# Attention denominators: sums on VectorE, one ones-product per chunk and head group, two context banks

## The chip, the cores and the metric

One core of one Trainium2 chip. The time is the device time of one execution in microseconds (us). Each of the eight sequences of the input ("batch" b below) runs through the whole layer; there is one launch.

## What is computed

For 8 sequences of 1,024 tokens and 256 features, in float32:

```
paths = sigmoid(x @ Wp + bp)                    # 8 heads x 5 values per token
agree = pq * pk + (1 - pq) * (1 - pk)           # per pair of tokens, head, depth
sim   = cumprod(agree, -1).sum(-1) / 5          # causal mask above the diagonal
attn  = softmax(sim, -1)
ctx   = attn @ V,  V = x @ Wv  (8 heads of 32)
x     = layernorm(x + ctx @ Wo)
h     = silu(x @ wg.T) * (x @ wu.T)             # hidden 768, integer weights / 127
x     = layernorm(x + h @ wd.T)
```

The similarity is a product of 32 features per token and head, so that the scores are a matmul. The softmax is written as exp without a maximum; its denominator is the sum of the probabilities over the keys.

## The kernel before

One list, `PLAN`, gives the order of all pieces of work. Each engine walks the same list and runs the pieces that are its own, in that order, and waits on semaphores. TensorE is PE, VectorE DVE, ScalarE ACT, GpSimd POOL.

Attention of a batch is 24 steps (`STEPS`). A step is one block of 128 keys (j) for one chunk of 512 queries (c) and one head group of 4 heads (g). The four pairs of chunk and group are q = 0 to 3: q 0 and q 1 (c = 0) have 4 steps each, i = 0 to 3 and 4 to 7; q 2 and q 3 (c = 1) have 8 each, i = 8 to 15 and 16 to 23. Only the queries from `off` on see a block: the four diagonal blocks of each chunk (`DIAG`) have 512, 384, 256 and 128 columns, the others 512.

Step s of the whole run (24 b + i) is planned as: `scores` (PE, L695) fills the two PSUM tiles `slot`; `exps` (ACT, L409) writes the probabilities of the 4 heads into one of three buffers `probs`; on the diagonal `mask` (POOL, L355) zeroes the 128 x 128 triangles; then come the pieces that `BETWEEN[i]` lists; then `weigh` for the step two before it (`LAG` = 2). `weigh` (PE, L717) has two groups of 4 matmuls, all over the same probabilities: the values `vz_sb` into `ctx_ps`, and a block of ones into `den_ps`, each head into its 32 partitions. After the last step of a q, `normalise` (DVE, L477 to L490) copies the context out of `ctx_ps`, transposes the denominators, takes the reciprocal, transposes back and multiplies into `ctxT`. So `normalise` stands in steps 5, 9, 17 and, for q 3, in step 1 of the next batch.

`BETWEEN` places the rest between the attention steps, one batch ahead (projections `vz`, `bias`, `squash`, `features`, `turn_f`, `phi` with `phi_low` on DVE) or one behind (`project` and `residual`, `stats` and `apply` of a layernorm with `rsqrt` on POOL, `turn_x1` with x1T_lo on DVE, the FFN's `gate`, `up`, `down`). A `gate_pair` is: gate (PE), tanh (ACT, L421), up (PE), and `hidden` on DVE, two instructions (L548, L556). `halves` is hid_hi (ACT, L427) and hidden_lo (POOL, L364), which `down` (PE, L762) waits for.

All PE pieces but scores and weighing write to two PSUM banks `misc` in turn. `MISC` numbers the uses in the order of `PLAN`, and a piece waits (`claim`) until its bank's last use is drained, mostly by a DVE instruction.

## Time and profile before

| | |
|---|---|
| median of 3 runs | 953.42 us (953.01 to 960.25) |
| the profiled execution, its own time | 955.83 us |
| its span, first to last instruction | 954.1 us |
| mean granted clock of TensorE | 0.969 |
| PE busy | 848.8 us, 89% |
| DVE busy | 478.6 us, 50% |
| ACT busy | 455.7 us, 48% |
| POOL busy | 227.4 us, 24% |

The busy times are of one profiled execution and are shares of its span. A busy PE is not PE at its peak: matmuls overlap, and their ends are modelled, so the cost of a group is read from its start to the start of what follows. PEclk is the granted clock as a share of 2.4 GHz; 0.5 is 1.2 GHz.

### The profile page before, as it was taken

What the parts mean: (1) busy time and instruction counts of PE and PEld (TensorE: products, weight loads), DVE (VectorE), ACT (ScalarE), POOL (GpSimd) and SP (SyncE); (2) the same over time, 40 slices, a digit from 0 to 9 for tenths busy, and PEclk for the clock granted to TensorE, in tenths of its full rate; (3) what the DMA queues carried; (4) which work ended last, traced back from release to release, by engine and by line L of the source; (5) the groups of instructions that cost most, each with busy time, mean ns of one, the idle gap of its engine ahead of it and who ended that gap; (6) DMA issues with size and microseconds to landing.
All of it is one profiled execution on the core that took longest, in us unless ns stands there. A gap on an engine that the chain in (4) does not pass through costs nothing.

```text
span 954.1 us, 15450 instructions
## 1 busy us (share of the span) xinstructions
PE 848.8 (89%) x6146; PEld 412.9 (43%) x6146; DVE 478.6 (50%) x1020; ACT 455.7 (48%) x721; POOL 227.4 (24%) x265
## 2 busy tenths in 40 slices
PE   4389998899989999899988999899988998999764
PEld 3144354443644446344544436344453434444332
DVE  2844346535455426645465355555275353545343
ACT  2255644555445554546445453555546453555211
POOL 0011131223212132122312232132321223231312
PEclk9599999999999999999999999999999999999968
DMA  6831443140511433113431406104321214100000
GB/s 211 213 97 45 89 89 111 45 90 23 141 59 45 111 66 107 72 43 70 89 111 45 89 23 152 70 23 111 82 74 45 64 48 109 47 1 23 1 22 24
DMA packets 44346, 71.09 MB, mean 75 GB/s; under 512 B 3568, under 2 KB 21232, under 8 KB 44272
## 3 DMA queue, kind: packets, MB, share of 16 engines
q1 hardware_dynamic: 44272, 70.07, 28.0%
q8 instruction: 51, 0.84, 0.4%
q14 instruction: 23, 0.19, 0.1%
HBM read 53.28 MB, written 16.78 MB: 73 GB/s over the span
## 4 chain that ended last, share of the span: by engine, by line
PE 73%; ACT 9%; DVE 9%; issue 4%; POOL 3%; DMA 2%; SPq 0%; POOLq 0%; ACTq 0%; DVEq 0%
PE ctx_ps L717 14%; PE misc L752 13%; PE den_ps L717 12%; PE slot L695 11%; PE misc L762 9%; PE misc L671 7%; PE misc L729 6%; ACT probs L409 6%; POOL work L364 2%; PE misc L680 2%; DVE work L548 2%; DVE x L531 1%; ACT work L421 1%; DVE ctx_raw L480 1%; DMA query_stack<-phi_dram 1%
## 5 line engine op out<-in xcount | busy, mean ns | idle before, releaser
L409 ACT ACTIVATE probs<-slot 128x1024 f32<-128x1024 f32 (+3 forms) x384 | 290.3, 808 | 376.4 <-PE slot L695 376.2
L695 PE MATMUL slot<-query_stack,key_stack 128*128 128x512 f16 (+3 forms) x768 | 161.7, 333 | 16.5 <-DMA query_stack<-phi_dram 15.1
L717 PE MATMUL ctx_ps<-probs,vz_sb 128*32 128x512 f32 (+3 forms) x1536 | 166.3, 505 | 10.3 <-DVE ctx_raw L480 8.3
L364 POOL TENSOR_TENSOR work<-work 128x512 f16<-128x512 f32 x96 | 112.7, 1174 | 216.0 <-ACT work L427 215.9
L717 PE MATMUL den_ps<-probs,ones 128*32 128x512 f32 (+3 forms) x1536 | 162.8, 495 | 0.0
L355 POOL TENSOR_SCALAR_AFFINE_SELECT probs<-probs 128x512 f32<-128x512 f32 x128 | 81.8, 641 | 303.9 <-ACT probs L409 302.9
L548 DVE SCALAR_TENSOR_TENSOR work<-work,misc 128x512 f32<-128x512 f32 x96 | 65.8, 686 | 172.7 <-ACT work L421 172.7
L752 PE MATMUL misc<-x1T_hi,w_parts 128*128 128x512 f16 x384 | 147.0, 383 | 5.2 <-DVE x1T_lo L538 2.4
L752 PE MATMUL misc<-x1T_lo,w_parts 128*128 128x512 f16 x384 | 146.5, 382 | 0.0
L695 PEld LDWEIGHTS slot<-query_stack,key_stack 128*128 128x128 f16 x768 | 56.8, 98 | 170.4 <-issue 120.9
L762 PE MATMUL misc<-w_parts,work 128*128 128x256 bf16 x768 | 89.1, 273 | 10.6 <-POOL work L364 10.6
L507 DVE SCALAR_TENSOR_TENSOR x<-misc,out_scale,x 128x512 f32<-128x512 f32 x32 | 24.0, 751 | 142.2 <-PE misc L762 142.2
L762 PEld LDWEIGHTS misc<-w_parts,work 128*128 128x128 f16 x768 | 73.7, 98 | 27.4 <-POOL work L364 16.4
L717 PEld LDWEIGHTS den_ps<-probs,ones 128*32 128x32 f32 x1536 | 50.2, 111 | 77.1 <-issue 68.1
L360 POOL TENSOR_TENSOR rstd<-var_eps,neg_half 128x4 f32<-128x4 f32 x32 | 32.4, 1013 | 193.7 <-DVE var_eps L525 193.7
L671 PE MATMUL misc<-wvp_sb,xT_sb 128*128 128x296 f32 x256 | 71.1, 425 | 7.3 <-DMA bp_sb<-in_bp_dram 7.3
L556 DVE SCALAR_TENSOR_TENSOR work<-work,hid_scale,misc 128x512 f32<-128x512 f32 x96 | 71.8, 748 | 3.8 <-PE misc L752 0.4
L729 PE MATMUL misc<-wo_sb,ctxT 128*128 128x256 f32 x256 | 60.9, 393 | 5.2 <-DVE ctxT L489 5.2
L421 ACT ACTIVATE work<-misc 128x512 f32<-128x512 f32 x96 | 57.8, 602 | 12.8 <-PE misc L752 12.8
L427 ACT ACTIVATE work<-work 128x512 f16<-128x512 f32 x96 | 61.3, 638 | 2.0 <-DVE work L556 2.0
L717 PEld LDWEIGHTS ctx_ps<-probs,vz_sb 128*32 128x32 f32 x1536 | 30.6, 108 | 72.5 <-issue 64.8
L752 PEld LDWEIGHTS misc<-x1T_hi,w_parts 128*128 128x128 bf16 x384 | 37.8, 98 | 55.7 <-DVE work L548 8.3
(52 smaller groups left out, 609.8 us busy)
## 6 DMA issues: line engine op xcount, KB each, us to landing
key_stack<-phi_dram SPq DMA_DIRECT2D x64, 256.0 KB, 5.8
query_stack<-phi_dram SPq DMA_DIRECT2D x64, 256.0 KB, 6.5
xT_sb<-in_xT_dram SPq DMA_DIRECT2D x8, 1024.0 KB, 5.1
x_sb<-in_x_dram SPq DMA_DIRECT2D x8, 1024.0 KB, 5.5
out_dram<-x SPq DMA_DIRECT2D x16, 512.0 KB, 2.9
phi_dram<-phi_hi SPq DMA_DIRECT2D x16, 256.0 KB, 2.0
phi_dram<-phi_lo SPq DMA_DIRECT2D x16, 256.0 KB, 2.3
work<-in_wgT_dram SPq DMA_DIRECT2D x1, 768.0 KB, 8.2
```

Of the source, the lines that this page charges most:

```text
L355: pool.affine_select(out=tile, in_=tile, compare_op=ALU.is_ge, fill=0.0, base=0, pattern=[[0, 4], [1, P]], channel_multiplier=-1).then_inc ...
L364: pool.tensor_tensor(hid_lo[:, n % M1, :], hid[:, n % HSLOTS, :], hid_hi[:, n % M1, :], ALU.subtract).then_inc(hid_lo_ready, 1)
L409: act.activation(probs[:, s % P_SLOTS, 2 * p:2 * p + 2, off:CH], slot[p][:, :, off:CH], ACT.Exp).then_inc(slot_drained[p], 1)
L421: act.activation(tanh_g[:, n % 2, :], misc[k][:, :], ACT.Tanh, scale=0.5 * QUANT).then_inc(tanh_ready, 1)
L548: dve.scalar_tensor_tensor(out=gated[:, n % 2, :], in0=tanh_g[:, n % 2, :], scalar=1.0, in1=misc[k][:, :], op0=ALU.add, op1=ALU.mult)\
L556: dve.scalar_tensor_tensor(out=hid[:, n % HSLOTS, :], in0=gated[:, n % 2, :], scalar=hid_scale[:, 0:1], in1=misc[k][:, :], op0=ALU.mult, o ...
L671: mm = pe.matmul(misc[k][:, 0:VZ], xT_sb[:, d, t * P:(t + 1) * P], wvp_sb[:, d, :], start=(d == 0), stop=(d == KD - 1))
L695: mm = pe.matmul(slot[p][:, k, off:CH], key_stack[:, h, P * j:P * (j + 1)], query_stack[:, h, CH * c + off:CH * (c + 1)], start=True, stop ...
L717: mm = pe.matmul(sums[32 * k:32 * k + 32, off:CH], w, probs[:, s % P_SLOTS, k, off:CH], start=first, stop=final)
L729: mm = pe.matmul(misc[k][:, (t % 2) * D:(t % 2 + 1) * D], ctxT[:, g, t * P:(t + 1) * P], wo_sb[:, g, :], start=(g == 0), stop=(g == NG - 1))
L752: mm = pe.matmul(misc[k][:, :], w_parts[:, w, e, d * F + m * P:d * F + (m + 1) * P], a[:, d, CH * c:CH * (c + 1)], start=(at == 0), stop=( ...
L762: mm = pe.matmul(misc[k][:, (t % 2) * D:(t % 2 + 1) * D], a[:, m, t * P:(t + 1) * P], w_parts[:, 2, e, m * D:(m + 1) * D], start=(at == 0) ...
```

## The change

- DVE gets a piece `sum` (`add_up`), planned in step s for the probabilities of step s - 1, ahead of the pieces of `BETWEEN`. The first sum of a q (j = 1) adds the probabilities of its first two steps into `acc` (on a diagonal step the columns below `off` are copied); each later one adds its step's to `acc`.
- PE's `weigh` loses the group over ones. A new piece `den`, behind the last weighing of a q, multiplies ones with `acc`, 4 matmuls into a `misc` bank; `normalise` transposes from there.
- `ctx_ps` becomes two banks, used in turn by q; the copy ctx_raw goes, and the last product of `normalise` reads `ctx_ps`.
- `exps` waits, beside `pv_done`, until the sum over the buffer that it overwrites is done.

```
@@ attention(s)
+        if 1 <= s <= B * NS:
+            plan += [("sum", *divmod(s - 1, NS))]
         plan += between(b, i)
         if LAG <= s < B * NS + LAG:
             b, i = divmod(s - LAG, NS)
-            plan += [("weigh", b, i)] + [("normalise", b, q) for q in range(NQ) if LAST[q] == i]
+            plan += [("weigh", b, i)]
+            for q in range(NQ):
+                if LAST[q] == i:
+                    plan += [("den", b, q), ("normalise", b, q)]
@@ the uses of misc
-        if what in ("scale", "vz", "turn_f", "project", "turn_x1", "gate", "up", "down"):
+        if what in ("scale", "vz", "turn_f", "project", "turn_x1", "gate", "up", "down", "den"):
@@ tiles
-        ctx_raw = sb("ctx_raw", [P, CH], F32)
+        acc = sb("acc", [P, 4, CH], F32)
-        ctx_ps = ctx.enter_context(nc.psum_tensor("ctx_ps", [P, CH], F32))
-        den_ps = ctx.enter_context(nc.psum_tensor("den_ps", [P, CH], F32))
+        ctx_ps = [ctx.enter_context(nc.psum_tensor(f"ctx_ps{n}", [P, CH], F32)) for n in range(2)]
@@ exps (ACT)
                     act.wait_ge(pv_done, s - P_SLOTS + 1)
+                    b2, i2 = divmod(s - P_SLOTS, NS)
+                    act.wait_ge(summed, SUMMED[b2, i2 + (STEPS[i2][3] == 0)])
@@ DVE
+            def add_up(b, i):
+                q, c, g, j = STEPS[i]
+                if j == 0:
+                    return
+                off = max(P * j - CH * c, 0)
+                s = NS * b + i
+                own = probs[:, s % P_SLOTS, :, off:CH]
+                if i in DIAG:
+                    dve.wait_ge(masked, len(DIAG) * b + DIAG.index(i) + 1)
+                else:
+                    for p in range(2):
+                        dve.wait_ge(slot_drained[p], s + 1)
+                if j == 1:
+                    if NQ * b + q >= 1:
+                        k, n = MISC[("den", *divmod(NQ * b + q - 1, NQ))]
+                        dve.wait_ge(misc_filled[k], n + 1)
+                    first = probs[:, (s - 1) % P_SLOTS, :, :]
+                    if off:
+                        dve.tensor_copy(acc[:, :, 0:off], first[:, :, 0:off]).then_inc(summed, 1)
+                    dve.tensor_tensor(acc[:, :, off:CH], first[:, :, off:CH], own, ALU.add).then_inc(summed, 1)
+                else:
+                    dve.wait_ge(summed, SUMMED[b, i] - 1)
+                    dve.tensor_tensor(acc[:, :, off:CH], acc[:, :, off:CH], own, ALU.add).then_inc(summed, 1)
@@ normalise (DVE)
-                dve.wait_ge(pv_done, NS * b + LAST[q] + 1)
-                if Q >= 1:
-                    dve.wait_ge(ctxT_ready, Q)
-                dve.tensor_copy(ctx_raw[:, :], ctx_ps[:, :]).then_inc(ctx_out, 1)
-                dve.transpose(den_turned[:, :, :].rearrange("p a n -> p (a n)"), den_ps[:, :]).then_inc(den_out, 1)
-                dve.wait_ge(den_out, Q + 1)
+                k, n = MISC["den", b, q]
+                dve.wait_ge(misc_filled[k], n + 1)
+                dve.transpose(den_turned[:, :, :].rearrange("p a n -> p (a n)"), misc[k][:, :])\
+                    .then_inc(misc_drained[k], 1)
+                dve.wait_ge(misc_drained[k], n + 1)
...
-                dve.wait_ge(ctx_out, Q + 1)
-                dve.tensor_tensor(ctxT[:, g, :], ctx_raw[:, :], den_inv[:, :], ALU.mult)\
+                dve.wait_ge(pv_done, NS * b + LAST[q] + 1)
+                dve.tensor_tensor(ctxT[:, g, :], ctx_ps[q % 2][:, :], den_inv[:, :], ALU.mult)\
@@ weigh and denominator (PE)
-                for sums, taken in ((ctx_ps, ctx_out), (den_ps, den_out)):
-                    if first and NQ * b + q >= 1:
-                        pe.wait_ge(taken, NQ * b + q)
-                    for k in range(4):
-                        h = 4 * g + k
-                        w = vz_sb[:, b % 2, j, 32 * h:32 * h + 32] if taken is ctx_out else ones[:, :]
-                        mm = pe.matmul(sums[32 * k:32 * k + 32, off:CH], w,
-                                       probs[:, s % P_SLOTS, k, off:CH], start=first, stop=final)
+                if first and NQ * b + q >= 2:
+                    pe.wait_ge(ctxT_ready, NQ * b + q - 1)
+                for k in range(4):
+                    h = 4 * g + k
+                    mm = pe.matmul(ctx_ps[q % 2][32 * k:32 * k + 32, off:CH],
+                                   vz_sb[:, b % 2, j, 32 * h:32 * h + 32],
+                                   probs[:, s % P_SLOTS, k, off:CH], start=first, stop=final)
                 mm.then_inc(pv_done, 1)
+
+            def denominator(b, q):
+                pe.wait_ge(summed, SUMMED[b, LAST[q]])
+                n = claim("den", b, q)
+                for k in range(4):
+                    mm = pe.matmul(misc[n][32 * k:32 * k + 32, :], ones[:, :], acc[:, k, :], start=True, stop=True)
+                mm.then_inc(misc_filled[n], 1)
```

`SUMMED` counts the increments of `summed` up to each step.

## Rows read from the trace of the kernel before

**Rows 1.** The page, part 1: busy us (share of the span) xinstructions.
```profile
PE 848.8 (89%) x6146; PEld 412.9 (43%) x6146; DVE 478.6 (50%) x1020; ACT 455.7 (48%) x721; POOL 227.4 (24%) x265
```
**Rows 2.** The page, part 4: the chain that ended last, by engine.
```profile
PE 73%; ACT 9%; DVE 9%; issue 4%; POOL 3%; DMA 2%; SPq 0%; POOLq 0%; ACTq 0%; DVEq 0%
```
**Rows 3.** Windows: batch 4 (steps 0-5, 6, 7-10, 11-14, 15-23), then batch 5.
```profile
core 0: us, PE busy (x) PEld busy (x) DVE busy (x) ACT busy (x) POOL busy (x), PEclk, DMA share, GB/s
461.34:489.43 28.09, 27.89 (x220) 17.61 (x216) 14.64 (x41) 12.00 (x21) 6.99 (x10) 1.00 0.52 131
489.43:497.70 8.27, 5.80 (x40) 2.61 (x37) 6.91 (x15) 3.56 (x7) 0.64 (x1) 0.84 0.38 127
497.70:516.76 19.06, 16.59 (x124) 6.89 (x120) 9.91 (x15) 11.46 (x17) 3.79 (x4) 0.98 0.15 56
516.76:535.20 18.44, 18.44 (x125) 8.42 (x121) 9.37 (x23) 9.98 (x15) 5.82 (x8) 1.00 0.00 1
535.20:573.05 37.85, 36.52 (x281) 15.59 (x277) 16.17 (x33) 19.69 (x30) 11.01 (x12) 1.00 0.31 73
573.05:683.11 110.06, 103.60 (x772) 50.78 (x769) 57.28 (x124) 56.68 (x90) 28.21 (x33) 1.00 0.30 77
```
**Rows 4.** Timeline of PE, batch 4: ahead of turn_features (step 6) and down (15).
```profile
493.39 1.22 PE L680 MATMUL misc<-ident,feat 128*128 128x128 f32 x8 [2.47 <-DVE x1T_lo L538]
...
536.29 2.79 PE L762 MATMUL misc<-w_parts,work 128*128 128x256 bf16 x24 [0.69 <-POOL work L364]
```
**Rows 5.** Timeline of PE: weighing of 128 and of 512 columns.
```profile
511.64 0.43 PE L717 MATMUL ctx_ps<-probs,vz_sb 128*32 128x128 f32 x8
511.88 0.40 PE L717 MATMUL den_ps<-probs,ones 128*32 128x128 f32 x8
...
514.91 1.06 PE L717 MATMUL ctx_ps<-probs,vz_sb 128*32 128x512 f32 x8
515.79 1.04 PE L717 MATMUL den_ps<-probs,ones 128*32 128x512 f32 x8
```
**Rows 6.** Groups by form, VectorE's longest tensor_tensor: busy us, mean ns | idle before.
```profile
L583 DVE TENSOR_TENSOR work<-work,w_parts 128x1536 f32<-128x1536 int32 x3 | 5.2, 1748 | 0.0
```
**Rows 7.** Timeline of VectorE in batch 4: statistics, normalise, apply, phi_low, hidden.
```profile
470.45 1.40 DVE L520 BATCH_NORM_STATS2 bn<-x 128x6 f32<-128x256 f32 x4
...
472.37 0.69 DVE L480 COPY ctx_raw<-ctx_ps 128x512 f32<-128x512 f32 x1
...
475.36 1.38 DVE L531 TENSOR_SCALAR x<-x,mv,rstd 128x256 f32<-128x256 f32 x4
...
512.47 0.75 DVE L470 SCALAR_TENSOR_TENSOR phi_lo<-misc,feat_scale,phi_hi 128x512 f16<-128x512 f32 x1 [0.75 <-ACT phi_hi L398]
...
530.94 0.75 DVE L556 SCALAR_TENSOR_TENSOR work<-work,hid_scale,misc 128x512 f32<-128x512 f32 x1
...
548.20 0.69 DVE L548 SCALAR_TENSOR_TENSOR work<-work,misc 128x512 f32<-128x512 f32 x1 [1.38 <-ACT work L421]
548.92 0.75 DVE L556 SCALAR_TENSOR_TENSOR work<-work,hid_scale,misc 128x512 f32<-128x512 f32 x1
...
570.03 0.75 DVE L556 SCALAR_TENSOR_TENSOR work<-work,hid_scale,misc 128x512 f32<-128x512 f32 x1
```
**Rows 8.** Mask and hidden_lo on GpSimd; hidden_lo beside a product of VectorE (timeline).
```profile
L355 POOL TENSOR_SCALAR_AFFINE_SELECT probs<-probs 128x512 f32<-128x512 f32 x128 | 81.8, 641 | 303.9 <-ACT probs L409 302.9
...
L364 POOL TENSOR_TENSOR work<-work x96: 1152/1162/1643, 107.7 to 938.9; 128x512 f16<-128x512 f32 x96
...
836.15 0.69 DVE L489 TENSOR_TENSOR ctxT<-ctx_raw,den_inv 128x512 f32<-128x512 f32 x1
836.22 1.64 POOL L364 TENSOR_TENSOR work<-work 128x512 f16<-128x512 f32 x1 [2.11 <-ACT work L427]
```
**Rows 9.** Timeline of batch 0: scores of step 4, end of the weights' split.
```profile
54.71 1.04 PE L695 MATMUL slot<-query_stack,key_stack 128*128 128x512 f16 x4
...
56.12 0.17 DVE L621 COPY w_one<-w_gmax 128x2 f32<-128x2 f32 x1 [1.54 <-issue]
```

More of the change, by code:

```diff
@@ L153, in seq_postln_kernel @@
             misc_uses[k] += 1
+    SUMMED, pieces = {}, 0
+    for b in range(B):
+        for i in range(NS):
+            q, c, g, j = STEPS[i]
+            pieces += (0, 2 if c == 0 else 1)[j >= 1] if j <= 1 else 1
+            SUMMED[b, i] = pieces
     NORM = {tuple(n): at for at, n in enumerate([n for what, *n in PLAN if what == "stats"])}
@@ L245, in seq_postln_kernel @@
         pv_done = sem("pv_done")
-        ctx_out = sem("ctx_out")
-        den_out = sem("den_out")
+        summed = sem("summed")
         den_recip_ready = sem("den_recip_ready")
@@ L472, in phi_low @@
                                          op0=ALU.mult, op1=ALU.subtract).then_inc(misc_drained[k], 1)
+            def add_up(b, i):
+                q, c, g, j = STEPS[i]
+                if j == 0:
[19 more added lines that the diff above has]
+                    dve.tensor_tensor(acc[:, :, off:CH], acc[:, :, off:CH], own, ALU.add).then_inc(summed, 1)
             def normalise(b, q):
@@ L633, in _ @@
                     split_weights()
+                elif what == "sum":
+                    add_up(*n)
                 elif what == "normalise":
@@ L779, in walk @@
                         weigh(*n)
+                    elif what == "den":
+                        denominator(*n)
                     elif what == "project":
```

## The prediction

> **What bounds the kernel now.** The page's busy times come first: TensorE is busy 849 of 954 us, VectorE half as long [rows 1], and the chain that ended last is 73% TensorE [rows 2]. That says where a removed instruction may pay, not how much. So I cut one batch in the middle of the run at the starts of score groups and read PE and DVE side by side [rows 3]. In steps 0 to 5 PE stops for 0.2 us, in steps 6 to 10 it stands still for 4.9 us, then it is nearly full again. The batch takes 111.7 us, the next one 110.1 us. The 1.6 us between them is low clock: steps 6 to 10 show a granted clock of 0.84 and 0.98 (of 2.4 GHz; a mix of 2.4 and 1.2), right behind PE's stop of 2.47 us, and the next batch shows 1.00 throughout. PE's stops name their releasers [rows 4]: the long one VectorE's x1T_lo, the one ahead of down GpSimd's hidden_lo. So PE sets the pace, but it runs through a ring of two `misc` banks, and VectorE, in program order, frees most of them. The change moves work from the first engine to the second.
>
> **What is removed on PE.** A full denominator group (4 heads of 512 columns) delays what follows as the context group ahead of it does, 515.79 - 514.91 = 0.88 us; one of 128 columns 0.24 us [rows 5]. On the line between them 384 columns cost 0.67 and 256 cost 0.45 us. A batch has 12 groups of 512 and 4 of each other size: 10.6 + 2.7 + 1.8 + 1.0 = 16.0 us. Added are four groups over `acc`, 4 x 0.88 = 3.5 us. Net 12.5 us a batch, 100 us in all, if nothing else came late.
>
> **What is added on DVE.** No row shows a tensor_tensor of 4 x 512. Two inputs in SBUF take 1,748 ns for 1,536 elements (L583) and 0.69 us for 512 (L489) [rows 6, 8]: 1.03 ns per element, so 2.28 us for 2,048, and 1.75, 1.22 and 0.69 us in the diagonal steps. A successor starts 0.03 to 0.09 us before the listed end [rows 7], so I use 2.25, 1.67, 1.15 and 0.62. Bounds of a full sum: 2.11 us at 1.03 ns without any start-up, 2.76 us at four times the 512-element row. I take the line, since the 1,536 row is nearest. The short head copy (512 elements) lies between half the 512 row, 0.35, and 0.69 us; I take 0.35, it is small either way. A batch has eight full sums, four of each shorter size and two copies: 18.0 + 6.7 + 4.6 + 2.5 + 0.7 = 32.5 us. Removed are four copies of ctx_raw at 0.6, 2.4 us. The final product now reads PSUM; the copy L480, as long, out of PSUM takes the same 0.69 us as L489 out of SBUF [rows 7, 8], so nothing. DVE goes from 57.3 us a batch [rows 3] to 87.4 us, PE from 103.6 to 91.1 us. The two become nearly equal, and where DVE's part of a step is longer than PE's, DVE sets the pace.
>
> **Where this lands in a batch.** I walked the batch in program order on both engines, always taking the later of "engine free" and "bank or data there" (0.1 us for a hand-over and 0.9 us where a tanh lies between are estimates). Start of a score group in us from the batch's own start, before [rows 3] and after:
> - Step 6: 28.1, after 28.0. Weighing loses 0.45, 0.24, 0.88, 0.67, 0.45, 0.24, and two denominators add 1.76: -1.2. Down of step 0 comes earlier on PE than hidden_lo on its chain of ACT and GpSimd: 1 us more of waiting. In step 2 the second `vz` wants the denominator's bank, which DVE's transpose frees only behind the layernorm statistics: a new stop of 0.85. Smaller hand-overs differ by -0.7.
> - Step 7: 36.4, after 35.3. PE waits for x1T_lo. DVE comes to it behind the normalise and, newly, behind the sum of step 5 (0.35 + 1.67): the stop grows from 2.5 to 3.7. Weighing loses 0.88, and the low clock no longer costs, as DVE is 2 us behind PE there.
> - Step 11: 55.4, after 52.9. Weighing loses 0.67, 0.45, 0.24 and 0.88, the second denominator adds 0.88; the rest is what the shorter `normalise` gives back.
> - Step 15: 73.9, after 71.5. This stretch becomes DVE's. From the end of phi_low (512.47 + 0.75) to the end of `hidden` of step 13 (530.94 + 0.75) it took 18.5 us with gaps [rows 7]. After: normalise 3.0 - 0.6 = 2.4, four full sums 9.0, three pairs of `hidden` at 0.72 + 0.66 = 4.1, residuals 1.2, statistics 1.9, apply 1.3 and 0.4 of hand-overs: 20.3 us without a gap. PE saves 3.5 us of weighing from step 11 to 15 and waits it all again, 1.4 us at step 11, 0.7 and 1.8 at steps 13 and 14.
> - End: 111.7, after 106.7. Steps 15 to 17 save 2.2 on weighing against 0.88 for the denominator and 0.9 more of waiting for hidden_lo. Then DVE again: from hidden(0) (548.92 + 0.75) to hidden(5) (570.03 + 0.75) it took 21.1 us [rows 7]; after it is apply 1.3, normalise 2.4, sums 9.0 + 1.67, five pairs 6.9 = 21.3 us. PE's saving there only brings the batch's end closer behind DVE's.
> So of 12.5 us removed, 3.4 us (110.1 to 106.7) remain against a batch without low clock, 4.2 against the mean of both.
>
> **The port.** GpSimd's hidden_lo, 1.16 us as a rule, took 1.64 us when it began 0.07 us behind L489, a VectorE product of two SBUF tensors, and L489 kept its 0.69 us [rows 8]. The second to come waited. Every sum is such an instruction. Mostly hidden_lo and mask will wait for the sum and then run beside `hidden`, which reads PSUM, at no cost. In the diagonal steps 20 to 22 and in 14 mask and hidden_lo are both queued behind the sum, 0.64 + 1.16 = 1.8 us against the pair's 1.4: the next sum waits 0.3 us, four times, and the last hidden_lo reaches down by so much later: 1.5 us a batch with its own waiting. The batch becomes 108.2 us.
> The Trainium skill says this outright ("SBUF — State Buffer", section "Who interferes with whom"): a VectorE instruction with two SBUF inputs and a GpSimd instruction that reads SBUF share an interface, and the later one blocks fully. By that rule, the trace agrees; were there no such lock, the batch would be 106.7 and the forecast 10 us lower.
>
> **The other edits.** Two context banks: the waits for ctx_raw at a new chunk go, but DVE sets the pace around them, so I take nothing for it; were they all on the path, it would be 1 us a batch. `exps` also waits for the sum of three steps back, and with it the next scores: late by 1.2 us at step 19, still ahead of PE's need. In batch 0 it costs: DVE splits weights until 56.3 us [rows 9]; the sum of step 1 ends at 58.3, exps(3) at 59.0, scores(4) starts at 59.1 instead of 54.7. The weighing saved in that batch outweighs these 4.4 us; I take -3 us for batch 0, between 0 and -8. Behind the last batch only a copy falls away, -0.6 us. More stops mean more low clock: at 1.6 us a period, mostly under DVE's work, I add 0.5 us a batch.
>
> **Sum.** Seven batches x (108.2 - 110.9) = -19, batch 0 -3, tail -0.6, clock +3.5: -19 us. The profiled execution took 955.8 us (span 954.1 and 1.7 around it), which gives 936.7. It lies 2.4 us above the median of the runs shown, so 953.4 - 19 = 934 us.
>
> **Rivals.**
> - *PE stays the bound* and DVE keeps up everywhere: 953 - 100 = 853 us. For it: a DVE that is half idle today. Against: the two stretches of 41.6 us have no room on DVE by rows. Chance 0.03. In part (sums at 2.11 us, no port waits) it gives 905 to 920: chance 0.05.
> - *The clock takes it back.* Stops of 1.4 to 1.9 us appear at steps 11, 14, 15 and 18 beside the 3.7. The stop of 2.47 us was followed by low clock in this batch and not in the next. If two such periods a batch are not covered, that is +3.2 us x 7, less the 3.5 counted: 953 us, no change. Chance 0.23.
> - *The port makes it slower.* One mechanism: in the eight steps that DVE bounds the sum finds hidden_lo (1.16 us) at the port, because hid_hi leaves ACT just ahead of the sum and not during it. Then GpSimd's time joins DVE's own chain: 8 x 1.0 us a batch, 934 + 7 x 8 = 990 us. It decides for slower from 4 us of such waits a batch. Against: ACT does exp and tanh first, so hid_hi ends some 0.5 us before the sum does. Chance 0.14.
> - That a denominator group stays in `weigh` is excluded by the diff, so the change does what it says.
>
> **Chances and range.** Forecast (920 to 944) 0.55, more gain 0.08, clock 0.23, port 0.14. A measurement of this kernel tells 1% (9.5 us) from no change. Faster by over 1%, below 943.9: 0.63; within 1%: 0.23; slower: 0.14. The range 914 to 963 leaves out the slower case and the free PE.
>
> **What would show it.** In the changed profile: PE busy down by some 100 us, DVE up by 230 to 240 us to about 715; a full sum at 2.28 us; steps 10 to 13 and 18 to 22 with DVE over 95% busy and PE waiting at `misc` for L548's product; the stop ahead of turn_features in step 6 at 3.7 us behind x1T_lo; batches of 107 to 110 us; hidden_lo often at 1.5 us and more; scores(4) of batch 0 near 59 us. Wrong it would be by sums much over 2.3 us, by DVE idle in those steps (then the ring binds, not the load), or by sums that start long after both inputs while GpSimd is busy.

## The result and the profile after

The changed kernel takes 978.18 us (median of 4 runs, 974.59 to 981.85) against 954.24 us for the kernel before beside it (953.01 to 960.25): 1.0238 times as long, 95% interval 1.018 to 1.0296. The forecast was 934 us in a range of 914 to 963; the change makes the kernel slower by 2.4%, 24 us, where 19 us of gain were forecast.

The page of the changed kernel, busy times and the chain that ended last by engine, which answer to [rows 1] and [rows 2]:
```profile
PE 793.5 (81%) x4866; PEld 379.8 (39%) x4866; DVE 737.0 (75%) x1164; ACT 459.7 (47%) x721; POOL 327.3 (34%) x265
...
PE 46%; DVE 21%; issue 11%; ACT 10%; POOL 9%; DMA 2%; SPq 0%; DVEq 0%; ACTq 0%; POOLq 0%
```
PE gave up 55 us and DVE took 258 us. What was not expected stands at the end of the first line: GpSimd runs the same 265 instructions and is busy 100 us longer. In the chain PE lost 27 points of share; DVE has 12 more, POOL 6 and "issue" 7.

The groups of GpSimd in the changed kernel show where the 100 us are:
```profile
L374 POOL TENSOR_TENSOR work<-work 128x512 f16<-128x512 f32 x96 | 145.3, 1514 | 208.8 <-ACT work L440 208.5
L365 POOL TENSOR_SCALAR_AFFINE_SELECT probs<-probs 128x512 f32<-128x512 f32 x128 | 132.5, 1037 | 244.2 <-ACT probs L422 244.2
L370 POOL TENSOR_TENSOR rstd<-var_eps,neg_half 128x4 f32<-128x4 f32 x32 | 51.1, 1597 | 182.7 <-DVE var_eps L563 159.2
```
hidden_lo took 1,162 ns in the median and mask 641 in the mean [rows 8]; now their means are 1,514 and 1,037. The reciprocal root of a layernorm works on 4 elements per partition; its mean was 1,013 ns and is 1,597 ns.

Windows over the changed kernel, in the same steps of batch 4 as [rows 3] (columns as there):
```profile
471.20:502.60 31.40, 28.77 (x189) 17.36 (x185) 20.94 (x47) 12.64 (x22) 9.88 (x11) 0.95 0.48 119
502.60:511.40 8.80, 5.07 (x32) 2.52 (x28) 7.53 (x13) 3.67 (x7) 0.64 (x1) 0.83 0.31 116
511.40:529.10 17.70, 15.19 (x101) 5.99 (x98) 12.69 (x19) 11.47 (x17) 3.14 (x3) 0.99 0.16 59
529.10:549.30 20.20, 17.27 (x93) 7.50 (x90) 19.74 (x29) 10.21 (x15) 13.11 (x8) 0.92 0.00 1
549.30:583.65 34.35, 31.46 (x216) 13.27 (x213) 28.16 (x39) 19.25 (x29) 15.39 (x11) 1.00 0.34 78
```
Against [rows 3], steps 0 to 5 take 3.3 us more, steps 11 to 14 1.8 us more with DVE busy 98% of them, and only steps 7 to 10 and 15 to 23 are shorter (by 1.4 and 3.5 us). Cut at the starts of score groups, batch 0 is 7.0 us longer than before (93.8 for 86.8), batches 1 to 6 together 9.3 us (674.6 for 665.3, so 112.4 each for 110.9), batch 7 up to its last scores 1.4 us, and what follows them, the tail, 5.2 us (67.7 for 62.5): 22.9 us, with the first scores 0.1 us earlier. The two spans differ by 22.8 us.

PE's longest waits in the changed kernel (us in total, times, longest):
```profile
PE misc L720 <- DVE x1T_lo L576: 22.4, 6, 3.7
PE misc L808 <- POOL work L374: 22.2, 14, 3.2
PE misc L784 <- DVE work L586: 17.1, 7, 2.9
PE misc L798 <- DVE work L586: 15.8, 20, 1.4
```

### The profile page after: what moved, and what is told of

It reads as the page before. It is cut to its first block, busy times and chain, and to the rows that moved or that the text cites. A ratio compares the mean times of both kernels' runs of the same rounds, so it can differ in the third digit from the quotient of the medians.

```text
span 976.9 us, 13193 instructions
## 1 busy us (share of the span) xinstructions
PE 793.5 (81%) x4866; PEld 379.8 (39%) x4866; DVE 737.0 (75%) x1164; ACT 459.7 (47%) x721; POOL 327.3 (34%) x265
## 4 chain that ended last, share of the span: by engine, by line
PE 46%; DVE 21%; issue 11%; ACT 10%; POOL 9%; DMA 2%; SPq 0%; DVEq 0%; ACTq 0%; POOLq 0%
PE misc L808 9%; PE ctx_ps L755 8%; ACT probs L422 7%; PE slot L735 7%; PE misc L711 6%; PE misc L798 6%; PE misc L775 5%; POOL probs L365 5%; DVE acc L508 4%; DVE work L586 4%; POOL work L374 3%; DVE x L569 2%; DVE acc L511 2%; DVE bn L558 2%; PE misc L720 2%
## 5 line engine op out<-in xcount | busy, mean ns | idle before, releaser
L511 DVE TENSOR_TENSOR acc<-acc,probs 128x2048 f32<-128x2048 f32 (+3 forms) x128 | 221.4, 1730 | 5.3 <-POOL probs L365 4.8
L374 POOL TENSOR_TENSOR work<-work 128x512 f16<-128x512 f32 x96 | 145.3, 1514 | 208.8 <-ACT work L440 208.5
L365 POOL TENSOR_SCALAR_AFFINE_SELECT probs<-probs 128x512 f32<-128x512 f32 x128 | 132.5, 1037 | 244.2 <-ACT probs L422 244.2
L755 PE MATMUL ctx_ps<-probs,vz_sb 128*32 128x512 f32 (+3 forms) x1536 | 175.4, 531 | 2.6 <-POOL probs L365 2.6
L808 PE MATMUL misc<-w_parts,work 128*128 128x256 bf16 x768 | 98.6, 290 | 22.4 <-POOL work L374 22.2
L370 POOL TENSOR_TENSOR rstd<-var_eps,neg_half 128x4 f32<-128x4 f32 x32 | 51.1, 1597 | 182.7 <-DVE var_eps L563 159.2
L586 DVE SCALAR_TENSOR_TENSOR work<-work,misc 128x512 f32<-128x512 f32 x96 | 65.4, 681 | 42.0 <-ACT work L434 42.0
L808 PEld LDWEIGHTS misc<-w_parts,work 128*128 128x128 f16 x768 | 78.5, 104 | 44.1 <-POOL work L374 28.3
L711 PE MATMUL misc<-wvp_sb,xT_sb 128*128 128x296 f32 x256 | 75.1, 438 | 10.8 <-DMA bp_sb<-in_bp_dram 7.0
L798 PEld LDWEIGHTS misc<-x1T_hi,w_parts 128*128 128x128 bf16 x384 | 38.1, 99 | 83.1 <-DVE work L586 31.9
L508 DVE TENSOR_TENSOR acc<-probs 128x1536 f32<-128x1536 f32 (+1 forms) x32 | 64.5, 2017 | 0.0
L711 PEld LDWEIGHTS misc<-wvp_sb,xT_sb 128*128 128x128 f32 x256 | 49.8, 202 | 31.1 <-DMA bp_sb<-in_bp_dram 7.1
```

The lines of the kernel that those rows point to most:

```text
L365: pool.affine_select(out=tile, in_=tile, compare_op=ALU.is_ge, fill=0.0, base=0, pattern=[[0, 4], [1, P]], channel_multiplier=-1).then_inc ...
L374: pool.tensor_tensor(hid_lo[:, n % M1, :], hid[:, n % HSLOTS, :], hid_hi[:, n % M1, :], ALU.subtract).then_inc(hid_lo_ready, 1)
L508: dve.tensor_tensor(acc[:, :, off:CH], first[:, :, off:CH], own, ALU.add).then_inc(summed, 1)
L511: dve.tensor_tensor(acc[:, :, off:CH], acc[:, :, off:CH], own, ALU.add).then_inc(summed, 1)
L586: dve.scalar_tensor_tensor(out=gated[:, n % 2, :], in0=tanh_g[:, n % 2, :], scalar=1.0, in1=misc[k][:, :], op0=ALU.add, op1=ALU.mult)\
L711: mm = pe.matmul(misc[k][:, 0:VZ], xT_sb[:, d, t * P:(t + 1) * P], wvp_sb[:, d, :], start=(d == 0), stop=(d == KD - 1))
```

## The experiments

All ratios are to the kernel before, run beside each. Its medians there were 954.3 to 955.8 us.

**What DVE's time costs, and what the port costs.** *One input.* The sums become reductions over the same number of elements, which read one SBUF tensor; the denominators are left out of the result (the matmul over ones reads a constant `acc`). The main line of the edit:
```
-dve.tensor_tensor(acc[:, :, off:CH], acc[:, :, off:CH], own, ALU.add).then_inc(summed, 1)
+dve.tensor_reduce(junk[:, 0:4], own, AX.X, ALU.max).then_inc(summed, 1)
```


> Each sum becomes a tensor_reduce over as many elements of the same buffer, with one input and a tiny output, so the denominators are left out (ones times a constant). VectorE's time and order stay (1,753 ns against 1,748 ns for 1,536 elements in the kernel before); the second SBUF input goes. Theory port (the sums keep GpSimd from the SBUF, and what GpSimd is late with stops down, apply and the next sum): mask, rsqrt and hidden_lo go back to 0.64, 1.01 and 1.16 us, the stop ahead of down in step 0 falls from 2 us to about 1, 925 to 950 us. Theory load (VectorE's 32 us more a batch, in program order, is enough): 970 to 985 us, as the changed kernel.

Measured: 953.59 us, ratio 0.9981 (0.9965 to 0.9997), 4 us above the range of theory port and 16 us below that of theory load. A reduction takes as long as a sum: its timeline row for 2,048 elements beside the one of the changed kernel, each with the reciprocal root that comes right behind it. The changed kernel (VectorE, then GpSimd, step 12 of batch 4):
```profile
537.37 2.29 DVE L511 TENSOR_TENSOR acc<-acc,probs 128x2048 f32<-128x2048 f32 x1
...
537.51 3.02 POOL L370 TENSOR_TENSOR rstd<-var_eps,neg_half 128x4 f32<-128x4 f32 x1 [2.57 <-DVE var_eps L563]
```
With one input (the same two, same step):
```profile
524.41 2.29 DVE L514 TENSOR_REDUCE junk<-probs 128x4 f32<-128x2048 f32 x1
...
524.55 1.01 POOL L372 TENSOR_TENSOR rstd<-var_eps,neg_half 128x4 f32<-128x4 f32 x1 [3.40 <-DVE var_eps L566]
```
GpSimd's groups of that kernel:
```profile
L376 POOL TENSOR_TENSOR work<-work 128x512 f16<-128x512 f32 x96 | 111.2, 1158 | 238.6 <-ACT work L442 237.8
L367 POOL TENSOR_SCALAR_AFFINE_SELECT probs<-probs 128x512 f32<-128x512 f32 x128 | 85.8, 671 | 279.7 <-ACT probs L424 279.7
L372 POOL TENSOR_TENSOR rstd<-var_eps,neg_half 128x4 f32<-128x4 f32 x32 | 32.4, 1012 | 190.9 <-DVE var_eps L566 167.4
```
Started 0.14 us behind a sum, the root stood until about the sum's end and then took its own time; behind a reduction it ran beside it. GpSimd is back near its old times, and 25 us are gone (978.2 to 953.6; by the two intervals 17 to 32). The reduction differs from the sum in its output too, 4 elements per partition for up to 2,048. That the second SBUF input is what counts shows in the changed kernel itself: 14 masks that began during the transpose den_inv (L523, one SBUF input, 512 columns written to SBUF) took 0.64 us, and the 7 hidden_lo that began during x1T_lo (L576, one input in SBUF and one in PSUM) took their 1.16 us. Masks that began during a `tensor_scalar` over SBUF (L569) took up to 0.85 us; that is open.

VectorE is held in its turn. DVE is busy 737.0 us in the change and 712.4 us here: some sums began while GpSimd was at work and took longer. In step 14 of batch 5 of the changed kernel (GpSimd, VectorE, PE):
```profile
655.12 1.16 POOL L374 TENSOR_TENSOR work<-work 128x512 f16<-128x512 f32 x1 [0.32 <-ACT work L440]
...
655.18 3.24 DVE L511 TENSOR_TENSOR acc<-acc,probs 128x2048 f32<-128x2048 f32 x1
...
659.17 1.08 PE L784 MATMUL misc<-ident,x 128*128 128x128 f32 x4 [2.90 <-DVE work L586]
```
The product of L586 stands behind that sum, and PE waits 2.90 us for it. Batches 2, 3, 5 and 6 are like this; in batches 1, 4 and 7 hidden_lo comes behind the sum, and PE's stop is 1.84 us, as with one input.

*No sums.* Each becomes a `memset` of one column; denominators left out.
```
+dve.memset(junk[:, 0:1], 0.0).then_inc(summed, 1)
```


> The changed kernel with each sum replaced by a memset of one column: the denominators are left out, TensorE's saving stays, VectorE's cost goes. If TensorE's 12.5 us a batch were simply on the path: 853 to 865 us. If GpSimd's and ACT's chains come next (hidden_lo ahead of down, x1T_lo): 870 to 895 us.

Measured: 885.96 us, 0.928 (0.9242 to 0.9319). So what PE gives up, with the second bank, is worth 69 us, and DVE's time takes 68 of them back, before the port (885.96 against 953.59).

*Sums that nobody reads*, added to the kernel before, with the wait of `exps`; its ones-groups and its one context bank stay. The line of the plan (the piece itself is that of the change):
```
+if 1 <= s <= B * NS:
+    plan += [("sum", *divmod(s - 1, NS))]
```


> The kernel before, with the sums beside it that nobody reads (and the wait of exps for them); the result is the reference's. Theory load: the same stretches become VectorE's with no saving on TensorE, 985 to 1000 us, far less than adding the two effects, since TensorE is hidden where VectorE bounds. If VectorE's cost and TensorE's saving add up (both all on the path): 978 + (954 - the time without sums), some 1050 to 1070 us.

Measured: 1042.97 us, 1.0907 (1.0879 to 1.0935), 87 us over the kernel before beside it, 7 us short of the range expected for adding up (1050 to 1070) and far from the other (985 to 1000). Had the two engines shared the load as a maximum, PE's untouched work would have covered a good part of that. It covered some 5 us at most: 978 us and the 69 us of PE's and the bank's saving make 1047. Costs on DVE and savings on PE add up almost as on one serial chain.

**Where the port hurts.** *Mask last*: the mask goes behind the pieces of `BETWEEN`, and so behind GpSimd's `hidden_lo` and root of its step. In the change it stands ahead of them, and in step 0 ahead of the split of the weights.
```
-if i in DIAG:
-    plan += [("mask", b, i)]
...
 plan += between(b, i)
+if b < B and i in DIAG:
+    plan += [("mask", b, i)]
```


> The changed kernel with GpSimd's mask planned behind the pieces of BETWEEN, so that hidden_lo and rsqrt of a step run ahead of it; nothing is left out. Theory port with the queue on GpSimd: hidden_lo of the last gate no longer stands behind a mask that a sum holds up, the stop ahead of down in step 0 falls from 2.0 to about 1.0 us, 966 to 973 us. Theory load: 975 to 982 us, or slower where the next sum waits for the later mask.

Measured: 968.18 us, 1.0133 (1.0101 to 1.0164). The 10 us come from batch 0 (93.8 to 89.2 us) and the tail (67.7 to 62.5, its length before the change); batches 1 to 6 keep their mean of 112.4.

The gain in batch 0 is not the port's. GpSimd also takes a maximum that DVE's split of the weights waits for (`w_gmax`), from values that DVE finishes at 45.6 us in both kernels. Planned behind mask(0) (44.04 to 44.68 us), it starts 8.2 us after that mask; planned ahead of it, as soon as DVE's values are there. First the changed kernel, then this one:
```profile
52.89 0.39 POOL L386 PARTITION_ALL_REDUCE w_gmax<-w_max  x1 [8.21 <-issue]
...
45.79 0.39 POOL L386 PARTITION_ALL_REDUCE w_gmax<-w_max  x1 [44.01 <-DVE w_max L627]
```
What GpSimd does in those 8.2 us the profile does not name ("issue"); the kernel before has such a gap too (7.4 us). So DVE is done with the weights 7 us earlier, the sums of q 0 end at 54.4 us and not at 61.5, and scores(4) starts at 54.69 us, as before the change.

In the changed kernel the tail begins so (GpSimd, then PE, timeline):
```profile
910.50 1.62 POOL L365 TENSOR_SCALAR_AFFINE_SELECT probs<-probs 128x512 f32<-128x512 f32 x1
912.09 1.15 POOL L374 TENSOR_TENSOR work<-work 128x512 f16<-128x512 f32 x1
...
913.29 0.94 PE L808 MATMUL misc<-w_parts,work 128*128 128x256 bf16 x7 [2.95 <-POOL work L374]
```
The sum of step 22 (910.21, 1.41 us) holds the mask of 0.64 us, `hidden_lo` stands behind it, and `down` behind that. The same order of events stands at every batch's start: in batch 5 GpSimd's rows and then PE's are
```profile
583.87 1.62 POOL L365 TENSOR_SCALAR_AFFINE_SELECT probs<-probs 128x512 f32<-128x512 f32 x1
585.47 1.15 POOL L374 TENSOR_TENSOR work<-work 128x512 f16<-128x512 f32 x1
...
586.67 4.46 PE L808 MATMUL misc<-w_parts,work 128*128 128x256 bf16 x24 [1.98 <-POOL work L374]
```
and `down` then runs at the low clock, 4.46 us for the 2.79 of [rows 4]. PE's stop there is 1.98 us in each of batches 1 to 7, 0.86 us with one input and 1.70 us with the mask last: with the mask out of the way the sum of step 22 holds `hidden_lo` itself (1.75 us in batch 5). So of the 1.1 us that the port adds to this stop, the queue behind the mask is 0.3. The low clock follows the stop in batches 2, 4 and 5 alone, where step 0 takes 8.0 us and not 6.3.

Means over batches 1 to 6 of the time from score group to score group, in us, put the places side by side:

| | before | change | one input | mask last | filled stops |
|---|---|---|---|---|---|
| step 0 | 4.96 | 7.15 | 5.19 | 6.03 | 6.32 |
| steps 1 to 5 | 23.13 | 23.39 | 23.40 | 24.16 | 23.40 |
| step 6 | 7.69 | 8.58 | 8.92 | 8.97 | 9.09 |
| steps 7 to 10 | 18.82 | 17.99 | 17.90 | 18.50 | 18.59 |
| steps 11 to 13 | 15.16 | 14.06 | 14.04 | 14.05 | 14.05 |
| step 14 | 3.27 | 6.71 | 5.78 | 5.15 | 5.85 |
| steps 15 to 23 | 37.85 | 34.53 | 34.39 | 35.52 | 35.24 |
| batch | 110.9 | 112.4 | 109.6 | 112.4 | 112.6 |

The port's 2.8 us a batch are 2.0 in step 0 and 0.9 in step 14. Mask last shortens the same two steps by 2.7 us together and loses as much in steps 5, 6, 7 and 15 to 23.

*Both last*: mask and sum behind the pieces, three buffers.
```
 plan += between(b, i)
+if b < B and i in DIAG:
+    plan += [("mask", b, i)]
+if 1 <= s <= B * NS:
+    plan += [("sum", *divmod(s - 1, NS))]
```


> Both changes of order together, mask and then sum behind the pieces of BETWEEN; nothing is left out. Theory place and port: the gains add, 930 to 948 us, which would beat the kernel before (954). Theory amount: 972 to 985 us.

Measured: 979.25 us, 1.0252 (1.0221 to 1.0282), no better than the change. With three buffers `exps` waits for the later sums (143 us in the run for 77), as in "sum last" below.

**The clock.** PE's time at the low clock (1.2 GHz) rose from 62 to 133 us; the mean granted clock fell from 0.969 to 0.933. *Filled stops*: 8 matmuls into the idle context bank ahead of `down` in step 0 and of `turn_x1` in step 14.
```
+def keep_busy(bank, done, times=8):
+    pe.wait_ge(ctxT_ready, done)
+    for n in range(times):
+        pe.matmul(ctx_ps[bank][:, :], w_parts[:, 0, 0, 0:P], w_parts[:, 1, 0, 0:CH], start=True, stop=True)
```


> The changed kernel with eight matmuls of 128x512 bf16 into the idle context bank ahead of the waits of down (step 0) and turn_x1 (step 14), 1.7 us in stops of about 2 us. Theory clock (the stops cost twice, because low clock follows them: the down group behind the stop took 4.46 instead of 2.79 us): low clock falls from 133 us to about 90 us in the run, 958 to 966 us. Port and load alone: 975 to 985 us.

Measured: 973.46 us, 1.0161 (1.0105 to 1.0218). The low clock is gone at both places. In step 14 of batch 4 `turn_x1` now runs at the full clock, and then PE waits anyway (PE's timeline):
```profile
541.83 1.89 PE L783 MATMUL ctx_ps<-w_parts 128*128 128x512 bf16 x8
544.90 0.63 PE L791 MATMUL misc<-ident,x 128*128 128x128 f32 x4 [1.18 <-DVE work L586]
...
548.75 2.79 PE L817 MATMUL misc<-w_parts,work 128*128 128x256 bf16 x24 [1.12 <-POOL work L374]
```
Batches 1 to 6 are not shorter (112.6 us for 112.4): steps 0 and 14 are 1.7 us shorter together, and steps 6 to 10 and 15 to 23 longer by 1.8. The 5 us in the median are within the two intervals. But the run did not take the low clock away. It came back behind step 6: the granted clock of that step of batch 4 is 0.76 for 0.83, and of the first 4 us of step 7 0.70. In all 119 of the 133 us at the low clock are left, where about 90 were expected. So this run does not show what the low clock costs.

**The wait of `exps`.** *Four buffers* of `probs` instead of three; `den_inv` shares `den_turned`'s memory to make room.
```
-P_SLOTS = 3
+P_SLOTS = 4
```


> The changed kernel with four buffers of probabilities instead of three, so that exps waits for the sum of four steps back; two denominator tiles share memory to make room. In the changed kernel ACT stands 77 us behind sums. Theory exps (these waits hold up the scores and so TensorE): 945 to 962 us. Port and load: no change beyond 5 us but for batch 0, whose 5 us of waiting behind the split weights shrinks: 970 to 978 us.

Measured: 978.88 us, 1.0241 (1.021 to 1.0272). Batch 0 becomes 90.0 us for 93.8, so the wait costs 3.9 us once; batches 1 to 6 and the tail stay. Batch 7 is 4.5 us longer up to its last scores (104.3 for 99.8), in steps 0, 3, 7 and 14; why is open.

*Sum last*: the sum goes behind the pieces, the mask stays.
```
-if 1 <= s <= B * NS:
-    plan += [("sum", *divmod(s - 1, NS))]
 plan += between(b, i)
+if 1 <= s <= B * NS:
+    plan += [("sum", *divmod(s - 1, NS))]
```


> The changed kernel with each step's sum planned behind the pieces of BETWEEN instead of ahead of them; nothing is left out. Theory place (the sum costs where it stands ahead of a piece that frees misc: x1T_lo in step 6, the gate products in steps 11 to 14 and 19): the stop ahead of turn_features falls from 3.7 to about 1.7 us and the one of step 14 by as much, 940 to 955 us. Theory amount (VectorE is full, it matters not which piece waits): 972 to 985 us.

Measured: 1010.66 us, 1.0579 (1.0544 to 1.0615). The waits of `exps` for sums, first in the changed kernel, then in this one:
```profile
ACT probs L422 <- DVE acc L508: 48.4, 25, 8.6
ACT probs L422 <- DVE acc L511: 28.9, 8, 4.2
```
```profile
ACT probs L422 <- DVE acc L508: 113.1, 31, 6.2
ACT probs L422 <- DVE acc L511: 58.4, 25, 7.4
```
The stretch of step 6, which had lost time to a sum ahead of x1T_lo, did shrink (5.5 us for 8.8), but `exps` waits 172 us for 77, and batches 1 to 6 take 115.9 us for 112.4. Most of that is step 0, 10.7 us for 7.2.

**The second context bank.** *One bank* and the copy ctx_raw again, all else changed.
```
+dve.tensor_copy(ctx_raw[:, :], ctx_ps[:, :]).then_inc(ctx_out, 1)
```


> The changed kernel with one context bank and the copy ctx_raw back in normalise; nothing is left out. It measures the part of the change that the forecast took for nothing: 976 to 984 us. Rival (the second bank and the missing copy are worth 1 us a batch and more, since VectorE is full): 986 to 995 us.

Measured: 1005.0 us, 1.0523 (1.0506 to 1.0541): 27 us slower than the change and above both expected ranges. Against the sums that nobody reads (1042.97 us, one bank as well) it is 38 us faster: that is what the removed denominator groups alone are worth beside the sums.

Batches 1 to 6 take 116.2 us for 112.4, and 2.7 of the 3.8 us are in step 19 (580.43 to 588.45 in batch 4, 8.0 us for 5.3). VectorE, then GpSimd, then PE in it:
```profile
577.10 0.68 DVE L522 COPY ctx_raw<-ctx_ps 128x512 f32<-128x512 f32 x1
...
580.09 3.25 DVE L510 TENSOR_TENSOR acc<-probs 128x2048 f32<-128x2048 f32 x1
583.26 0.67 DVE L592 SCALAR_TENSOR_TENSOR work<-work,misc 128x512 f32<-128x512 f32 x1
...
580.00 1.18 POOL L376 TENSOR_TENSOR work<-work 128x512 f16<-128x512 f32 x1 [5.44 <-ACT work L442]
...
583.99 0.39 PE L804 MATMUL misc<-x1T_hi,w_parts 128*128 128x512 f16 x1 [2.52 <-DVE work L592]
```
The copy puts 0.6 us into DVE's queue, the sum behind it begins 0.09 us behind a `hidden_lo` and takes 1.0 us longer than its 2.28, and PE's gate, which needs the product of L592 behind it, waits 2.5 us for 1.4. What follows is at the low clock; the window of step 19 here and then in the change:
```profile
580.43:588.45 8.02, 5.50 (x25) 1.38 (x21) 7.95 (x7) 3.06 (x4) 2.13 (x2) 0.79 0.01 2
...
566.29:571.60 5.31, 3.87 (x24) 1.17 (x21) 5.27 (x4) 2.95 (x4) 3.16 (x2) 1.00 0.01 3
```
From the gate's start to the next scores it is 4.5 us for 2.8: of the 2.7 us, 1.1 are the wait and 1.6 the rows at the low clock behind it. In the changed kernel the same first sum of a pair took 2,283 ns in the mean of 16, here 2,705.

**A better order.** *Four buffers, both last*: the two edits of "both last" and "four buffers" together.
```
-P_SLOTS = 3
+P_SLOTS = 4
...
 plan += between(b, i)
+if b < B and i in DIAG:
+    plan += [("mask", b, i)]
+if 1 <= s <= B * NS:
+    plan += [("sum", *divmod(s - 1, NS))]
```


> Mask and sum behind the pieces of BETWEEN, and four buffers of probabilities, so that the late sum no longer stops exps (172 us of waiting with three); nothing is left out. Theory place: with exps free the order helps, 940 to 958 us. Theory amount (VectorE's 32 us cost two thirds of what TensorE saves wherever they stand): 970 to 985 us.

Measured: **943.06 us**, 0.9865 (0.9847 to 0.9882), faster than both kernels. Windows over the same steps of batch 4:
```profile
450.85:483.48 32.63, 28.98 (x189) 17.27 (x185) 22.59 (x48) 12.52 (x22) 12.15 (x12) 0.95 0.48 116
483.48:488.98 5.50, 3.77 (x33) 2.19 (x29) 4.29 (x8) 3.51 (x7) 0.64 (x1) 1.00 0.43 170
488.98:508.13 19.15, 15.29 (x100) 5.75 (x97) 15.26 (x24) 11.51 (x18) 2.96 (x3) 1.00 0.15 56
508.13:525.48 17.35, 15.57 (x93) 7.24 (x89) 16.61 (x25) 9.98 (x15) 9.47 (x6) 1.00 0.00 0
525.48:559.43 33.95, 31.27 (x216) 13.44 (x212) 30.02 (x42) 19.46 (x30) 16.18 (x11) 1.00 0.36 80
```
Steps 6 and 11 to 14 are 3.3 and 2.9 us shorter than in the change and stay at the full clock; steps 0 to 5 are still the long ones (32.6 us for 28.1 before).

Four more tell what carries it. *Four buffers, sum last* (the mask in its old place):


> The changed kernel with four buffers and the sum last, the mask in its old place; nothing is left out. Theory place with exps as what stopped the late sum: four buffers are enough, 943 to 952 us. Theory port (the mask ahead of hidden_lo is held up by the sum and holds up down): 955 to 970 us.

Measured: 972.9 us, 1.0197 (1.0143 to 1.025), above both expected ranges. So the mask's place is worth 30 us here: 3.2 us in each of batches 1 to 6, above all in steps 0 and 14, and 5.3 us in the tail. *The kernel before with four buffers*, and *with four buffers and the mask last*:


> The kernel before with four buffers of probabilities and nothing else. Control for the version with both orders and four buffers (943 us): if that gain is the change's, given the right place, 950 to 958 us here; if the fourth buffer itself brings it, 938 to 948 us.

> The kernel before with four buffers and GpSimd's mask behind the pieces of BETWEEN; nothing is left out. Second control: 948 to 958 us if neither buffer nor order of GpSimd helps a kernel without sums; 938 to 946 us if hidden_lo ahead of mask brings down (0.2 to 0.7 us of waiting per batch) and more forward.

Measured: 955.37 us, 1.0007 (0.9991 to 1.0022), and 953.01 us, 0.9991 (0.9968 to 1.0013). Neither the buffer nor both together are worth anything without the sums, so the 1.35% are the change's own. *The better order with one-input sums* (denominators left out, as above):


> The version with both orders and four buffers, its sums replaced by tensor_reduce with one SBUF input (the denominators are left out). What is left of the port in it: theory port, 12 to 25 us, 918 to 931 us, with the stop ahead of down in step 0 back under 1.5 us; rival (the new order already keeps sums and GpSimd apart): 937 to 944 us.

Measured: 909.02 us, 0.953 (0.95 to 0.9559): the port still costs 34 us in the better order, more than the 12 to 25 expected.

**Fewer sums.** From the kernel before (one context bank, `den_ps` kept): sums for part of the steps, the others keep their ones-group. *q 0 and the first five steps of q 3*, then *the first five of q 3 alone*. The steps of each q that are summed:
```
+M = {0: 4, 1: 0, 2: 0, 3: 5}
...
+M = {0: 0, 1: 0, 2: 0, 3: 5}
```


> From the kernel before: VectorE sums only the four steps of q 0 and the first five of q 3, and one product over the sum takes the place of their ones groups; q 1, q 2 and the last three steps of q 3 keep theirs; one context bank and the copy stay. TensorE loses 4.9 us a batch, VectorE gains 13. Theory map (a sum costs only where it stands ahead of x1T_lo or a gate product that TensorE waits for: steps 6, 11, 14 and, for 1.6 us, 19): 936 to 946 us, faster than before. Theory amount (every us on VectorE costs 0.33 us, every us off TensorE gives 0.7): 960 us.

> As the one with q 0 and q 3, but only the first five steps of q 3: TensorE loses 3.5 us a batch, VectorE gains 9. Theory map: 2.6 us saved less 1.6 at step 19, 944 to 950 us. Theory amount: 957 to 961 us.

Measured: 972.18 us, 1.016 (1.0131 to 1.0188), and 963.7 us, 1.0085 (1.0057 to 1.0113). Both were placed where the one-input and the no-sums kernel, compared step by step, had shown little cost of DVE's time, and both lose, each by more than either theory had expected. In the second, step 19 of batch 4 takes 9.5 us for the 4.7 before, with PE in front of a gate:
```profile
559.33 0.61 PE L811 MATMUL misc<-x1T_hi,w_parts 128*128 128x512 f16 x1 [3.06 <-DVE work L593]
```
DVE there does `normalise`, a sum and only then the product that frees the bank, and the gate runs at the low clock. With this fell the idea that a half-idle DVE makes a sum free, even in chosen steps. Whether another choice of steps would gain was not tried.

## Why the prediction was wrong

The forecast lay 44 us below the result, 42 if the spans are compared. By the score groups, 26 of these are in batches 1 to 7 (112.4 us each where 108.7 were forecast, the 0.5 for the clock included), 10 in batch 0 and 6 in the tail. The steps that failed are the port, batch 0, the tail, and the low clock behind step 6; the bank was mis-sized in the good direction. By its own steps:

**The second bank, "I take nothing for it", "1 us a batch" at most.** Bank and copy together are worth 27 us beside the sums. The copy's own time, 2.4 us of DVE a batch, was in the walk; for the rest I took nothing, since I bounded it by the waits for ctx_raw in the trace of before, where no sum stood beside the copy on DVE. This error hides a part of the others: without bank and copy the change would have been at 1005 us. How the 27 us divide into the copy's time, PE's wait, the collision and the low clock was seen in step 19 and not measured apart.

**The port, 1.5 us a batch.** The mechanism was right, its size was not, and its place only in part. It cost 25 us between the medians and 23 us between the spans (976.9 against 953.7) where the sum had 10: 3.9 in batch 0 and 3.0 in the tail, for both of which I had nothing, and 16.9 in batches 1 to 6, 2.8 each. I looked for it in steps 14 and 20 to 22, where DVE sets the pace. Step 14 has 0.9 us of it, steps 20 to 22 0.2. The larger part, 2.0 us, is at the seam of two batches, where DVE is not the bound at all: the sum of step 22 holds mask(23) and hidden_lo, PE has nothing else in its order and waits for the last hidden_lo at `down` in step 0 (1.98 us for 0.86), and in batches 2, 4 and 5 it then runs `down` at the low clock. I had written the sentence ("the last hidden_lo reaches down by so much later") and given it a share of 1.5 us. And I had left GpSimd's root out: I thought of it as 4 elements, but at a locked port what counts is what is left of the other's instruction, here up to 2.3 us. Every GpSimd instruction of the profile before was a candidate; I priced hidden_lo and mask, in five steps.

The Trainium skill ("SBUF — State Buffer", section "Who interferes with whom") calls the shared ports an exclusive lock. By that rule, the trace agrees: 3.02 us for the root, 3.25 us for the sum in the one-bank kernel, each its own time (1.01 and 2.28) and about what was left of the other's (2.15 and 1.09).

**DVE sets the pace from step 11 on.** Right. DVE's chain from phi_low's end to `hidden` of step 13 was 20.3 us in the sum and is 20.46 in the one-input kernel (from 512.80 to 533.26), from hidden(0) to hidden(5) it was 21.3 and is 21.4 in the change (562.24 to 583.67); full sums are 2.28 us where nothing holds them, DVE is busy 98% in steps 11 to 14 (97% in steps 10 to 13, 99% in 18 to 22), and PE waits at `misc` for the product of L586. DVE's busy time without the port is 712.4 us (forecast 715).

**"The low clock no longer costs" behind step 6.** Wrong, and it is the largest part of what is left. Without the port the walk had 106.7 us a batch and the one-input kernel takes 109.6. Its windows over the same steps of batch 4:
```profile
460.93:489.53 28.60, 27.10 (x189) 16.50 (x185) 19.59 (x46) 12.62 (x22) 7.69 (x10) 1.00 0.53 131
489.53:498.48 8.95, 5.11 (x32) 2.54 (x29) 7.63 (x13) 3.67 (x7) 0.64 (x1) 0.83 0.35 114
498.48:516.14 17.66, 15.14 (x100) 6.03 (x97) 12.18 (x19) 11.47 (x17) 3.13 (x3) 0.99 0.16 59
516.14:536.29 20.15, 17.23 (x93) 7.49 (x89) 19.68 (x29) 10.21 (x15) 7.14 (x8) 0.92 0.00 1
536.29:570.45 34.16, 31.51 (x216) 13.34 (x213) 27.25 (x39) 19.30 (x30) 9.94 (x11) 1.00 0.34 78
```
The walk had 28.0, 7.3, 17.6, 18.6 and 35.2. Two stretches are longer, step 6 by 1.65 and steps 11 to 14 by 1.55 us, and both hold the low clock (0.83 and 0.92). In step 6 PE stops for 3.73 us in the changed kernel, as forecast (3.7), and then:
```profile
507.95 1.68 PE L720 MATMUL misc<-ident,feat 128*128 128x128 f32 x8 [3.73 <-DVE x1T_lo L576]
509.56 1.94 PE L755 MATMUL ctx_ps<-probs,vz_sb 128*32 128x512 f32 x8
```
The weighing had 1.06 us in [rows 5]. ScalarE and DVE turn to phi only when turn_features ends, so its slowness is on DVE's path as well. I had argued that DVE was 2 us behind PE there; at that point DVE waits for PE. In steps 11 to 14 the rows at the low clock stand behind PE's last stop; DVE does not wait there, and the next stretch is 1.0 us shorter than the walk had it, so little of those 1.55 us reaches the batch. That the low clock costs some 1.3 us in step 6 is read from these rows (1.68 us for 1.22, 1.94 for 1.06), not from a run that removed it alone; no filler was tried in step 6.

**Batch 0, -3.** It was +7.0. Scores(4) starts at 59.55 us (forecast 59.1, before 54.71), so the wait of `exps` was sized well; a fourth buffer gives back 3.9 us and one-input sums 3.9. What was wrong is the saving that should outweigh it. With no sums the batch takes 83.1 us, so PE's and the bank's saving is 3.7 us there and not the 7.4 that I set against the wait of 4.4; and the sums cost it 10.7 us in all, of which I had counted only that wait. The wait of scores(4) itself hangs on `w_gmax` standing behind mask(0): with the mask last it is gone.

**The tail, -0.6.** It was +5.2. All of it goes when the mask stands behind the last hidden_lo (62.5 us), and 3.0 us of it with one-input sums. I had walked no step behind the last scores.

**PE's 100 us.** PE's busy time fell by 55 us in the change, 87 us with no sums, where less of it is at the low clock. In time saved, PE's groups and the bank together came to 69 us, and the groups alone, beside the sums, to 38 us. That the rest went into waits for DVE, which PE had before too [rows 4], is argued, not measured.

**The rivals.** Of the three, "the port makes it slower" named the right sharer and the right side, 990 us for 978. Its collision, a sum that finds hidden_lo at the port, is in the change, in step 14 of batches 2, 3, 5 and 6, and DVE is busy 25 us longer in all (737.0 against 712.4 us), some 3 us a batch where the rival had 8. But the larger harm comes by GpSimd's queue to PE, which the rival had not. That its time lies near the measured one is in part luck, since bank, batch 0 and tail were off as well. "The clock takes it back" saw the low clock double, from 62 to 133 us. Whether it is cause or consequence stays open: the filled stops left 119 us of it, and so did the one-input kernel, which is 25 us faster. The general error is under all of them: I walked one batch on two engines and put GpSimd in as a correction. Three engines hand work to each other here, and the experiment with unread sums shows how little slack there was.

Open: what the low clock costs in a run, how the two readings of step 19 carry over to the other places, why the partial sums lose as much as they do beyond the one step shown, and whether the 5 us of the filled stops are real.

## What to carry to other kernels

Before moving work to an engine that is half idle, read how its queue stands between the others: here 234 us of added VectorE work cost 68 us, as much as the removed TensorE work and the second bank gave, and another 25 us came by the port, through a GpSimd that was 24% busy. A long two-input VectorE instruction prices every GpSimd instruction that begins during it, however small, and one that finds GpSimd at work is held itself; walk GpSimd's queue as its own engine, above all where the pipeline turns from one batch to the next. Give added work a place behind what others wait for, and the buffer that this place needs: from 978 us, the buffer alone gave 979, the sum's place alone 1011, the mask's alone 968 (half of that gain by an earlier `w_gmax`), all three together 943 us.

## What the hardware showed that was not expected

- A GpSimd instruction on 4 elements per partition took 3.02 us when it began 0.14 us behind a VectorE sum of 2,048 elements, and 1.01 us behind a reduction of the same length. The same happens to VectorE: its sum took 3.25 us when a GpSimd product had begun 0.09 us ahead of it.
- Masks that began during a VectorE transpose from SBUF to SBUF, or during a VectorE product with one input in PSUM, kept their 0.64 us; those that began during a sum, with two inputs in SBUF, took up to 2.15 us.
- A reduction over one SBUF input takes as long as the addition of two, 2.29 us each for 2,048 elements in float32, and leaves GpSimd alone.
- GpSimd's partition reduction `w_gmax` began 8.2 us after a mask and 7.3 us after its input was there; with no mask ahead of it, it began 0.1 us after its input.
- Eight matmuls of 512 columns ahead of turn_x1, the last of them ending 1.2 us before it, kept it at the full clock (0.63 us for four of 128 columns; in the change all eight took 1.87 us at the low clock).
